# A two-layer network on one core: the next batch of the first layer is routed ten slots sooner, and its scatter heads the round

## The reference: what is computed

```python
x = L0_attn_x
xn = _layernorm(x, axis=-1)
s = _L0_attn_ref(xn, L0_attn_wq, L0_attn_wk, L0_attn_wv, L0_attn_wo)
g = _silu(_L0_ffn_ref(xn, L0_ffn_Wg, L0_ffn_W1, L0_ffn_W2, L0_ffn_W3))
x = x + s * g
xn = _layernorm(x, axis=-1)
s = _L1_attn_ref(xn, ...)
g = _silu(_L1_ffn_ref(xn, ...))
x = x + s * g
```

## Time and profile before, and how to read them

| | us |
|---|---|
| median of 3 runs | 1364.67 |
| lowest, highest | 1358.96, 1369.6 |
| the profiled execution, its own time | 1365.29 |
| its span, first to last instruction | 1363.5 |
| mean granted TensorE clock | 0.868 |

### The profile page before, as it was taken

How to read it: one execution, slowest core, us unless ns; L and a number is a source line. 1 busy time by engine, 2 the same in 40 slices (tenths; PEclk the granted TensorE clock), 3 DMA queues, 4 the chain that set the end, 5 groups by cost and what they waited for, 6 DMA issues and landing times. The chain is left out here.

```text
span 1363.5 us, 24768 instructions
## 1 busy us (share of the span) xinstructions
PE 997.6 (73%) x7728; PEld 804.2 (59%) x7728; DVE 878.3 (64%) x2899; ACT 630.9 (46%) x1431; POOL 679.2 (50%) x750
## 2 busy tenths in 40 slices
PE   1668789677777686786787659989687877969712
PEld 0656666556656565666566337679476765867611
DVE  3334677766766777777667535380759669687794
ACT  0314434324234244243333227787686676767711
POOL 2022335545645664664556450714656556665565
PEclk9988889789888898798898758999798989989865
DMA  7594753534633733634543937977556756657522
GB/s 240 161 322 140 264 165 98 167 135 152 216 113 114 243 133 97 210 127 128 174 143 110 373 104 225 320 228 215 157 172 194 228 156 201 205 168 230 148 88 60
DMA packets 178783, 242.88 MB, mean 178 GB/s; under 512 B 20016, under 2 KB 110832, under 8 KB 178032
## 3 DMA queue, kind: packets, MB, share of 16 engines
q1 hardware_dynamic: 158192, 199.55, 45.0%
q0 software_dynamic: 20480, 41.98, 10.6%
HBM read 129.73 MB, written 111.74 MB: 177 GB/s over the span
## 5 line engine op out<-in xcount | busy, mean ns | idle before, releaser
L1441 POOL DMA_INDIRECT y<-y_rows,idxy x256 | 259.4, 1013 | 203.7 <-DMA y<-y_rows,idxy 74.3
L1361 POOL DMA_INDIRECT rows<-xs,idx x256 | 253.6, 991 | 69.9 <-issue 65.4
L2034 DVE SCALAR_TENSOR_TENSOR V<-y,w8all,V 128x128 f32<-128x128 f32 x232 | 82.5, 356 | 114.6 <-PE V L1080 98.5
L977 PE MATMUL U<-ident,xg 128*128 128x128 f32 x576 | 98.6, 298 | 60.6 <-ACT xT L1240 46.4
L1653 DVE TENSOR_TENSOR att<-X,causal 128x512 f32<-128x512 f32 x128 | 82.3, 685 | 84.0 <-PE X L793 45.0
L977 PEld LDWEIGHTS U<-ident,xg 128*128 128x128 f32 x576 | 69.8, 151 | 85.8 <-issue 70.9
L1204 ACT ACTIVATE wd<-GY 128x384 f32<-128x384 f32 x120 | 59.0, 492 | 120.2 <-PE GY L903 120.1
L1341 POOL TENSOR_TENSOR ppause<-neg_half 128x1 f32<-128x1 f32 x80 | 16.8, 210 | 191.9 <-DVE idx L1813 98.5
L1240 ACT ACTIVATE xT<-U 128x512 f32<-128x512 f32 x144 | 86.4, 600 | 19.2 <-PE U L977 19.0
L1334 POOL TENSOR_TENSOR rs<-rs,neg_half 128x4 f32<-128x4 f32 x16 | 16.7, 1044 | 140.7 <-DVE rs L1479 140.7
L1829 DVE SCALAR_TENSOR_TENSOR terms<-pp,p 128x160 f32<-128x160 f32 x256 | 83.5, 381 | 0.8
(11 more groups left out here) (325 smaller groups left out, 2501.7 us busy)
## 6 DMA issues: line engine op xcount, KB each, us to landing
xg<-rows SPq DMA_DIRECT2D x144, 256.0 KB
y_rows<-ys SPq DMA_DIRECT2D x144, 256.0 KB
wd<-in_w0e SPq DMA_DIRECT2D x56, 576.0 KB, 5.5
rows<-zero SPq DMA_DIRECT2D x25, 1024.0 KB, 5.5
rows<-zero SPq DMA_DIRECT2D x4, 3072.0 KB, 14.7
wd<-rows SPq DMA_DIRECT2D x8, 1024.0 KB, 8.8
y_rows<-wd SPq DMA_DIRECT2D x24, 256.0 KB, 3.0
wd<-in_wd SPq DMA_DIRECT2D x1, 5120.0 KB
```

Of the source, the lines that this page charges most:

```text
L977: last = nc.tensor.transpose(XT[:, q * P:(q + 1) * P], xg[:, k % RX, q, :], ident[:])
L1361: pool.indirect_dma_start(rows, bass.IndirectOffsetOnAxis(ap=idx[:, t * 8 + k:t * 8 + k + 1], axis=0), xs1[:, t, :], None)\
L1441: pool.indirect_dma_start(y8[:, i % RG, k, :], None, y_d[0:groups * Q * P, :], bass.IndirectOffsetOnAxis(ap=idxy[:, b, t * 8 + k:t * 8 + k ...
L2034: ins = nc.vector.scalar_tensor_tensor(o, y[:, k, :], w, o, ALU.mult, ALU.add)
```

## The change

Four things change, all in the first layer.

- **Ten slots sooner.** norm0a goes from 58 to 48, norm0b from 61 to 51, xn0_T and copy from 66 and 67 to 56 and 57, router0 and exp0 from 76 to 66, topk0a from 79 to 70, topk0b from 83 to 77; rot from 48 to 43.
- **Ranks and places at the round's end.** rank0 from slot 1 of the next round to 86, place0a, b, c from 4, 5, 7 to 87, 88, 89. They become steps of class pre1, so their semaphore counts rise by one batch.
- **shift0 is cut in two.** Its copy of the weights stays at slot 3 as shift_w; the copies of idx0 and ew go to slot 86 of the round before, as shift0 of class pre2, which now waits until this round's gather0 has landed.
- **POOL's order.** scatter0 goes from slot 10 to slot 0, ahead of both powers. The row scatters' parts are 3, 1, 4 in place of 3, 2, 3: scatter_b has one part and scatter_c four.

In LAST_STEPS only the name shift0 becomes shift_w; with the new NEW_PARTS its scatter_c at slot 12 has 16 DMAs in place of 12.

```diff
--- before.py
+++ after.py
@@ -138,13 +138,13 @@
                      (49 + 10 * t, "scores_a"), (50 + 10 * t, "mask_a"), (52 + 10 * t, "scores_b"), (53 + 10 * t, "mask_b"),
                      (55 + 10 * t, "av")):
         ATTENTION.setdefault(at, []).append((name, t))
-STEPS = {0: ["res_comb"], 1: ["res_silu", "rank0"], 2: ["res_gate"], 3: ["res_add", "shift0"], 4: ["place0a"], 5: ["place0b"], 6: ["res_norm"],
-         7: ["place0c"], 9: ["res_r1"], 10: ["scatter0"], 11: ["xn1_T", "xn1T_copy"], 12: ["router1", "scatter_c"], 13: ["probs1"], 14: ["place0d"],
+STEPS = {0: ["res_comb", "scatter0"], 1: ["res_silu"], 2: ["res_gate"], 3: ["res_add", "shift_w"], 6: ["res_norm"],
+         9: ["res_r1"], 11: ["xn1_T", "xn1T_copy"], 12: ["router1", "scatter_c"], 13: ["probs1"], 14: ["place0d"],
          15: ["topk1a"], 18: ["topk1b"], 20: ["topk1c"], 21: ["rank"],
          22: ["place_a"], 25: ["place_b"], 27: ["place_c"], 31: ["place_d"], 35: ["place_e"], 39: ["place_f", "xn1_copy"], 40: ["scatter"],
-         44: ["table"], 48: ["rot"], 58: ["norm0a"], 61: ["norm0b"], 64: ["gather0"], 65: ["scatter_b"], 66: ["xn0_T"], 67: ["xn0T_copy"],
-         76: ["router0", "exp0"], 79: ["topk0a"], 83: ["topk0b"]}
-LAST_STEPS = {0: ["res_comb"], 1: ["res_silu"], 2: ["res_gate"], 3: ["res_add", "shift0"], 6: ["res_norm"], 9: ["res_r1"],
+         43: ["rot"], 44: ["table"], 48: ["norm0a"], 51: ["norm0b"], 56: ["xn0_T"], 57: ["xn0T_copy"], 64: ["gather0"], 65: ["scatter_b"],
+         66: ["router0", "exp0"], 70: ["topk0a"], 77: ["topk0b"], 86: ["rank0", "shift0"], 87: ["place0a"], 88: ["place0b"], 89: ["place0c"]}
+LAST_STEPS = {0: ["res_comb"], 1: ["res_silu"], 2: ["res_gate"], 3: ["res_add", "shift_w"], 6: ["res_norm"], 9: ["res_r1"],
               11: ["xn1_T", "xn1T_copy"], 12: ["router1", "scatter_c"], 13: ["probs1", "topk1a"], 14: ["topk1b"], 15: ["topk1c"], 16: ["rank"],
               17: ["place_a"], 18: ["place_b"], 21: ["place_c"], 22: ["place_d"], 25: ["place_e"], 26: ["place_f", "xn1_copy"], 27: ["scatter"],
               30: ["table"], 64: ["gather0"], 65: ["scatter_b", "scatter_d"]}
@@ -158,10 +158,10 @@
        "topk1a", "topk1b", "topk1c", "rank", "place_a", "place_b", "place_c", "place_d", "place_e", "place_f", "table", "weights_a", "weights_b",
        "xn1_copy", "scatter", "scatter_b", "scatter_d"}
 
-PRE1 = {"norm0a", "norm0b", "xn0_T", "xn0T_copy", "router0", "exp0", "topk0a", "topk0b"}
-PRE2 = {"rank0", "place0a", "place0b", "place0c", "place0d", "scatter0", "rot"}
+PRE1 = {"norm0a", "norm0b", "xn0_T", "xn0T_copy", "router0", "exp0", "topk0a", "topk0b", "rank0", "place0a", "place0b", "place0c"}
+PRE2 = {"shift0", "place0d", "scatter0", "rot"}
 LATE = {"scatter_c"}
-NEW_PARTS = {"scatter": (0, 3), "scatter_b": (3, 5), "scatter_c": (5, 8)}
+NEW_PARTS = {"scatter": (0, 3), "scatter_b": (3, 4), "scatter_c": (4, 8)}
 
 SMALL_FROM = 29
 
@@ -1558,7 +1558,7 @@
                 dve.wait_ge(*seen.next("chosen0_ready"))
                 link(nc.vector.tensor_tensor(pl0[:], pl0[:], chosen0[:], ALU.mult))
                 for j in range(RW0):
-                    upto(dve, f"w0_in{j}", weights_in(here[0], j))
+                    upto(dve, f"w0_in{j}", weights_in(here[0] + 1, j))
                 nc.vector.tensor_scalar(ewn[:], ejr0[:], float(E0 - 1), None, ALU.min).then_inc(r0["ew_ready"], 1)
 
             def s_place0c(t):
@@ -1574,7 +1574,7 @@
                 join()
                 link(nc.vector.scalar_tensor_tensor(pos0_r[:], pos0_p[:], float(Q - 1), pos0[:], ALU.mult, ALU.add))
                 join()
-                upto(dve, "scat0", (here[0] + 1) * (16 * 2 * T))
+                upto(dve, "scat0", (here[0] + 2) * (16 * 2 * T))
                 nc.vector.scalar_tensor_tensor(idx0n[:], pos0_q[:], 1.0 - P, pos0_r[:], ALU.mult, ALU.add).then_inc(r0["idx0_ready"], 1)
 
             def s_place0d(t):
@@ -1588,17 +1588,21 @@
                 join()
                 link(nc.vector.tensor_tensor(w20n[:], w20n[:], sm0[:].unsqueeze(2).broadcast_to([P, T, 2]), ALU.mult))
 
-            def s_shift0(t):
-
-                upto(dve, "took0", here[0] * 128)
+            def s_shift_w(t):
+
                 upto(dve, "comb_in", here[0])
                 upto(dve, "comb_ready", here[0])
+                join()
+                link(nc.vector.tensor_copy(w20[:], w20n[:]))
+
+            def s_shift0(t):
+
+                upto(dve, "took0", here[0] * 128 + 128)
                 for j in range(MORE0 - RW0, MORE0):
-                    upto(dve, f"w0_in{j % RW0}", weights_in(here[0] - 1, j))
-                upto(dve, "idx0_ready", here[0] + 1)
-                upto(dve, "ew_ready", here[0] + 1)
-                join()
-                link(nc.vector.tensor_copy(w20[:], w20n[:]))
+                    upto(dve, f"w0_in{j % RW0}", weights_in(here[0], j))
+                upto(dve, "idx0_ready", here[0] + 2)
+                upto(dve, "ew_ready", here[0] + 2)
+                join()
                 link(nc.vector.tensor_copy(idx0[:], idx0n[:]))
                 join()
                 nc.vector.tensor_copy(ew[:], ewn[:]).then_inc(r0["shift0_ready"], 1)
```

More of the change, by code:

```diff
@@ L1589, in s_place0d @@
                 link(nc.vector.tensor_tensor(w20n[:], w20n[:], sm0[:].unsqueeze(2).broadcast_to([P, T, 2]), ALU.mult))
-            def s_shift0(t):
-                upto(dve, "took0", here[0] * 128)
+            def s_shift_w(t):
                 upto(dve, "comb_in", here[0])
                 upto(dve, "comb_ready", here[0])
-                for j in range(MORE0 - RW0, MORE0):
-                    upto(dve, f"w0_in{j % RW0}", weights_in(here[0] - 1, j))
-                upto(dve, "idx0_ready", here[0] + 1)
-                upto(dve, "ew_ready", here[0] + 1)
                 join()
                 link(nc.vector.tensor_copy(w20[:], w20n[:]))
+            def s_shift0(t):
+                upto(dve, "took0", here[0] * 128 + 128)
+                for j in range(MORE0 - RW0, MORE0):
+                    upto(dve, f"w0_in{j % RW0}", weights_in(here[0], j))
+                upto(dve, "idx0_ready", here[0] + 2)
+                upto(dve, "ew_ready", here[0] + 2)
+                join()
                 link(nc.vector.tensor_copy(idx0[:], idx0n[:]))
```

## The result

| | before | after |
|---|---|---|
| median, us | 1367.13 (4 runs) | 1408.80 (4 runs) |
| lowest, highest | 1358.96, 1374.91 | 1405.91, 1414.26 |
| profiled execution, own time | 1365.29 | 1406.97 |
| its span | 1363.5 | 1405.2 |
| mean granted TensorE clock | 0.868 | 0.858 |

A forecast was written before the change was run, and what follows sets the result against it. No engine is full; the order in each round's 90 slots, a dependent chain, sets its length. 25.7 - 20.9 + 23.9 + 2.8 + 5.2 + 7.2 + 4 = 47.9 us, hence 1412.6 us, range 1384 to 1432.

The forecast's parts named there:

- step D: Round 0: place0b's wait for a weight load moves to the round before, ahead of hs0; +2.8 us, bounds 0 and 8.
- Step E: Round 7: four more scatters move the landing before place_f later, with no scatter0 moved away; +5.2 us, bounds 3 and 7.
- the clock: Low PE clock goes behind norm0b, where the attention chain feels it; +4 us, bounds 0 and 11 in five rounds.
- Step F: Router and softmax ten slots sooner: copy +1.2, tables +1.3, old place -1.3; 7.2 us in six rounds, bounds 0 and 15.
- Step A: Round's start: scatter0 ahead of the two powers on POOL makes res_norm late; +25.7 us in six rounds, bounds 18 and 31.
- Step B: place_f no longer waits for row scatters, which start sooner behind the second power; -20.9 us, at least -14.
- The margin of 1.6 us: Before place_f: last landing seen at res_norm + 28.7, work in front ending at res_norm + 30.3, so the wait goes.
- Step C: norm0a at slot 48: its power stands behind twelve row scatters, delaying norm0b and mask_b; +23.9 us, bounds 17 and 29.
- the first: Rival: POOL's queue is the round's length, so idle time behind absorbs the new stalls; 1344 us, chance 0.07.
- The second: Rival: POOL reaches the powers in time at the round's start, so that cost is 0; 1387 us, chance 0.13.
- the third: Rival: place_f waits again for 2 us in five rounds and the clock takes its 11; 1430 us, chance 0.14.

The follow-up runs named there:

- Run 1: The changed kernel with scatter0 back at slot 10, behind both powers, and the row scatters split 3, 3, 2: 1375.84 us, ratio 1.0082.
- run 2: The changed kernel with norm0a at slot 36 in place of 48, ahead of the row scatters of slot 40: 1378.69 us, ratio 1.0102.
- run 4: The kernel before with the row scatters split 3, 3, 2 in place of 3, 2, 3, nothing else: 1348.79 us, ratio 0.9873.
- run 9: The kernel before with row scatters split 3, 3, 2 and round -1's three weight loads issued early: 1345.49 us, ratio 0.9854.
- run 3: The changed kernel with router0, exp0, topk0a and topk0b back at slots 76, 76, 79 and 83: 1403.51 us, ratio 1.0281.
- run 6: The kernel before with row scatters split 3, 1, 4, on a chip where the kernel before takes 1705.67 us: ratio 0.9977.

## Why the prediction was right

The forecast was 1412.6 us, 47.9 over the kernel before; the median is 1408.8, 41.7 over. The mechanism (a wait given back, two larger ones put in DVE's list) is what the runs show; step D had the wrong sign, and the sizes of E, of the clock and of two parts of F were off. That the sum came within 6.1 us is in part luck: by the rows of the table D and E came out 11.1 us below the forecast, and the row of F and the clock 6.4 above it.

- **Step A, scatter0 ahead of the powers: right.** +21.6 us in its segment, and 5.1 by which the last product itself is put off: 26.7 against 25.7. Run 1 takes scatter0 away from there and finds 27.2 us; the 5.6 between this and 21.6 are the early places, which shorten the segment in rounds 1, 2 and 6. The prediction had put these wholly inside the wait.
- **Step B, place_f: right.** -22.5 against -20.9. The margin of 1.6 us was thinner than stated: the landing is seen 5.9 and 5.5 us behind the last issue in rounds 3 and 4 of the changed kernel and not 5.0, and DVE waits 0.89 and 0.17 us again.
- **Step C, norm0a behind the row scatters: right.** +26.4 against 23.9. The five waits are 5.19, 6.77, 5.91, 6.77 and 5.94 us; run 2, which moves nothing but the asking, gets 31.1 us back in these five rounds, 27 in the medians. Without the wait mask_b comes about 1 us sooner behind place_f than in the kernel before; whether that is a gain isn't shown, as the same segment varies from 14.0 to 16.9 us between rounds of runs 4 and 9.
- **Step D, round 0: wrong sign**, -6.0 in place of +2.8. I followed DVE's wait for weights to its new place in DVE's list and left the time at which the loads are issued as it was. But SP issues them behind its own wait for xn0, and xn0 was itself moved. Three rows of the changed kernel, DVE's norm0b of round -1, SP's loads and ewn:

```profile
37.67 1.11 DVE L1484 TENSOR_SCALAR xn<-xs,mv,rs 128x128 f32<-128x128 f32 x4 [9.48 <-DMA rows<-xn,idx0n]
...
40.88 11.64 SPq L550 DMA_DIRECT2D wd<-in_w0e  x3
...
63.66 0.17 DVE L1562 TENSOR_SCALAR ewn<-ejr 128x7 int32<-128x7 f32 x1
```

  In the kernel before they are

```profile
51.56 1.11 DVE L1484 TENSOR_SCALAR xn<-xs,mv,rs 128x128 f32<-128x128 f32 x4 [1.24 <-POOL rs L1334]
...
55.95 9.42 SPq L550 DMA_DIRECT2D wd<-in_w0e  x3
```

  The loads start 15.1 us sooner, ewn waits no more, and PE's own wait for weights ends at 78.51 and not at 87.22, 8.7 us sooner. Early loads alone, run 9 against run 4, give 3.4 of these. The other 5.3 were not tested apart: the places no longer stand between the pages' products on DVE, which come some 2 us sooner than in run 9 (one at 72.03, there at 73.91), and the next loads on SP are issued at 70.75, in run 9 at 76.80. And of the -6.0 at the end of round 0 some 3.4 may be the stretch of low clock that the kernel before had in its profiled execution and run 4 had not. That there is no cost is sure, the size of the gain is not.
- **Step E, round 7: sign right, size too large**, +2.9 against 5.2. From res_norm to place_f round 7 is 2.0 us longer, the other 0.9 come behind it. I took the landing to follow the last issue by 5 us, as in round 3. Here it is 1.4 us (issue ended at 775.61, place_f at 777.03):

```profile
774.32 1.29 POOL L1361 DMA_INDIRECT rows<-xs,idx  x1 [0.30 <-issue]
777.03 0.06 DVE L1805 MEMSET pause<- 128x1 f32 x1 [2.25 <-DMA rows<-xs,idx]
```

- **Step F: right in sum by luck; the clock: too small.** The segment is +17.6 us against 11.2. Where both kernels have a granted clock of 1.00, its parts can be told one by one. The copy costs 0.95 in its new block (9.49 us in round 0 of the changed kernel and in run 2, against 8.54; taken 1.2) and its leaving gives 1.3 back in the block where it was (9.87 in round 3 before, 8.53 in run 3). The tables cost 2.5 and not 1.3, since both loads are exposed, and taking exponential and tables out of the last block gives 1.2. That is +0.9 a round where +1.2 was taken: the tables were mis-sized by 1.2, and the -1.3 that was taken once for what leaves is there twice. Another 0.7 a round is the last product put off, which belongs to A. The rest is the clock. Beyond these steps the first interval takes 1.1 us more in each of rounds 1 to 5 (1.3 in round 1) and the last 1.2 to 1.4, some 12 us in all, against 3.2 us that the kernel before lost in rounds 4 and 5 (11.48 us at 0.85 in place of 9.87). So the clock costs some 9 us more than before and not 4, within the bounds of 0 and 11. The 2.2 us at half speed for one block's chain, on which the bounds rest, were worked out from no row; the rows show 1.1 us at 0.76 to 0.84 in the first interval and 1.3 at 0.83 to 0.85 in the last.

The Trainium skill, "ScalarE: Activation LUTs", section "What ACT_TABLE_LOAD costs", would have had a drain of some 1380 ns at each switch. The rows of the changed kernel shown with run 3 speak against it once more: load end 425.99 + 1.28 = 427.27, activation 427.29.

Of the rivals, the first (POOL's queue is the round) is refuted on an ordinary chip, where each stall before norm0b made its segment longer by about its own length: the five are 30.6 us, and run 2 without them gets 31.1 back. On the other kind of chip, where moving whole parts changes nothing, it isn't refuted, but the changed kernel as it stands was not run there. The second needed A to be zero; A is 21.6 and more. Of the third, the clock came true in large part (9 of its 11 us), the renewed waits of place_f did not (1.1 us in place of 10).

## What to carry to other kernels

A short instruction that another engine waits for must not be queued behind a row of indirect DMAs: each took 1.27 us of POOL to issue, and a power of 1 us asked for behind eight to twelve of them cost DVE 3.0 to 6.8 us at each of two places in a round, more than the wait that the reordering removed. Before moving a step, look at which queue entries of every engine it passes, and also at which waits of the DMA-issuing engine it releases sooner: that was the one sign this prediction had wrong. When a wait is for DMAs that end late, first try to put fewer of them in front of it; one number in the split gave 1.3%, the whole reordering cost 3.3%. And before calling a step or the clock the cause of a longer stretch, compare the same instructions at the same granted clock: only so did the gain of the exponential's leaving and the price of the clock come apart here.

## What the runs showed of the hardware beyond this

- The time from the end of an indirect scatter's issue to its landing as DVE sees it is no constant: 4.4 to 5.1 us in rounds 2 to 6 of the kernel before, 5.9 and 5.5 in rounds 3 and 4 of the changed one and 1.4 in its round 7.
- A kernel can be 25 to 27% slower on one chip than on another (1364 to 1366 us on two of them, 1706 and 1733 on two others), though DVE, ACT and POOL are busy for the same time within 2%. PE is busy for 1084 to 1106 us there in place of 998, at a mean granted clock of 0.79 to 0.80 in place of 0.868, and the second layer, in which this copy has no part, takes 659 us in run 6 where it takes 561: some 100 of the 338 us more. What makes these chips slow is open. On them a page's copy in the first layer waits until POOL's row of scatters is issued, some 5.5 us more per four scatters. That the store which it waits for doesn't land meanwhile is read from the code; the landing itself isn't in the trace.
- In the changed kernel DVE waits for POOL at res_norm only 3.0 to 3.6 us in rounds 3 to 5, the rounds behind a jump back of the loop, against 6.5 to 6.8 in rounds 1, 2 and 6. In those three it is idle for 3.1 to 3.3 us ahead of res_comb, which the trace puts down to nothing but issue, in rounds 1, 2 and 6 for 0.24 at most. A stall of the same length in another queue therefore costs less at the seam of a loop.
- The granted clock shows plainly in the attention's intervals: the same instructions take 8.53 us at 1.00 and 9.8 at 0.83 to 0.85 (last interval), 9.87 at 1.00 and 11.48 at 0.85 (second interval, kernel before). A stall that is taken away can move the low clock to a later interval in place of ending it (run 2).
